# The shifted cross attention of an twelve-block decoder kernel: one head pipeline over four items instead of one per item

## The chip, the cores and the metric

The kernel runs on one core of one Trainium2 chip as one program. The metric is device microseconds (us) of one execution, the median of several. TensorE (PE, with its weight load PEld), VectorE (DVE), ScalarE (ACT), GpSimd (POOL) and SyncE (SP, whose queue issues nearly all transfers) each run their own instruction list in order and meet at semaphores.

## The reference, cut to what matters

Twelve blocks follow each other: attention, cross attention and feed-forward, in four layers, on x of 8 x 256 x 128. The change touches the cross attention of layer 1, a head attention with relative positions: the position scores `bd` are computed against all 512 positions and then shifted left row by row.

```python
def left_shift(x):
    L = x.shape[-2]
    M = x.shape[-1] - L
    flat = x.reshape(x.shape[:-2] + (-1,))
    i = jnp.arange(L)[:, None]
    j = jnp.arange(M)[None, :]
    i = jnp.arange(L)[:, None]
    j = jnp.arange(M)[None, :]
    idx = 2 * L - 1 + i * (M + L - 1) + j
    out = flat[..., idx]
    keep = j - i <= M - L
    return jnp.where(keep, out, jnp.zeros((), dtype=x.dtype))
...
ac = jnp.einsum('bhtd,bhsd->bhts', qh + b_u[None, :, None, :], kh)
bd = jnp.einsum('bhtd,hmd->bhtm', qh + b_v[None, :, None, :], ph)
scores = (ac + left_shift(bd)) / math.sqrt(D_K)
attn = jax.nn.softmax(scores, axis=-1)
out = jnp.einsum('bhts,bhsd->bthd', attn, vh).reshape(b, t, H_SIZE)
return out @ w_o
...
```

q is the layer norm of x, k and v are `ctx_1024`, and the result is added to x. There are 16 heads of width 8, and 8 batch items; positions and keys number 512 and 256, and no key is masked out.

## The kernel before

The 8 items form two streams of four (`streams`, `ITEMS` = 4); stream 0 holds the even items. Each stream has its own buffers, semaphores and four PSUM banks: S0, S1, T, V. For each engine a Python generator per stream walks the twelve blocks (the "own" walk), and a second one per stream runs ahead and prepares the next block's operands (the "ahead" walk, the `front` functions). `alternate` (line 2955) merges these four walks of an engine into one instruction list: the string `TURNS[engine]` says how many steps each walk takes in turn. So the order on every engine is fixed by those strings; a wait holds up everything behind it on that engine, of both streams.

In the shifted stage (`L1_xattn`, block 4) an item goes through these steps:

- **Front** (ahead walk, `front`, `front_norm`): layer norm, transposes, q, k and v matmuls, all in bank S1. ACT and DVE cut q with either bias and k into three bf16 pieces (`split_q`, `split_k`); SP stores them to HBM (`stack_out`, tile `stacks`) and reads them back in the layout of the matmuls (`stack_back`): `qv` (a tile `region` or `qv`, double buffered), then `qs` and `kz`, of which a stream has one copy each. So line 2745 lets SP wait until all 16 heads of the item before are scored, and then reads `qs` (96 rows of 4 KB) and `kz` (2 x 48 rows).
- **Shear**: for head h, PE multiplies `qv` with the positions into S1 (`shift`), ACT copies it to SBUF, and for each pair of heads SP stores it to HBM (`skew<-region`, two transfers) and reads it back with a row pitch one element shorter (`skew_room<-skew` and `P<-skew` in turn, two slots a stream), which is the left shift.
- **Head**: five heads behind the shear. PE forms the scores in S0, DVE adds the shifted part and takes the maximum (line 2090), ACT exponentiates (`P<-P,negm`), PE transposes into T (line 1153), DVE copies T out (line 2160), and every four heads PE weighs v into V.
- **End** (`finish`): PE transposes the 16 heads' results into T and V (line 912), DVE takes the sums and divides (lines 2164, 1976, 1838), PE transposes (line 888), ACT copies, PE projects into S0, DVE adds to x.

An item's loop (line 1171 on PE) runs `h` from 0 to 22: the last 7 rounds have no shear, and the first 5 have no head. Then comes the end, and only then, in the same walk, the first shear of the stream's next item. The ends of the two streams' items stand less than half an item apart in the lists.

Of the kernel before, what the change touches and what calls it, by code (L numbers as in the profile page):

```python
# [12 lines left out]
ALU = mybir.AluOpType  # L13
# [4 lines left out]
TOK = S // 128  # L18
# [34 lines left out]
    "tensor": ("0100110012003211110011001300130021002100210021002100110011001300140062002100210022001500210031002100120021001200"  # L53
        "2300120040010011001001020010101100100201001101003100110010010010220011003100110011001100111011001100210033002200"
        "1100210011001300110011003100420041001110010021100200110020010100101011001100120020101300100112001001010021002101"
        "0200110012002300110012001100410010100100202011001100321021002300110021001001410030011001010011001001010011001200"
        "1200210041003100220012001100410012001100110021003100120034002100130011001100110041001100130014001100330013001300"
        "2100110021001200110033001200110011003100110012002100210011001100120021005400110011002100120023001200210021002100"
        "1200230012001200210031001100110011001200260031001200230041001200130011001200110011004200440032001200130011001100"
        "3200210012002100120022003100120023006100120024001100110011001200230041001200240011002200310012002200220032001200"  # L60
        "1400210031001100230023003200330032001100510012001200120011001100110012001100120043002300110011002200310011001100"
        "3300110022001200130011001100310011001100120021001200220031001200110012006100120024001200210012002300410012002400"
        "1100120011004200230010100120020101030010610021002300120011004300110041003200120021001100210011002100220012002100"
        "2300110022001200110011003100110011001100210012001100211010100100211011002100110020102200120020011100100101021100"
        "1400110023002100410012001100120011001200210022002100130012001200110021001100210031002100210011001100210011001100"
        "1100210012003200210022001100220011001100120011002100120021001210010010100110120011001100111001001300130012003101"
        "1100100112020300430021001100130011002100310011002100110011002100120011002400140012002100120011002100210021002200"
        "3100410012001200110021002100130011001100210011001300110011001100110021001010212012002010020021001100120011001100"
        "1100210013002200110210010200220101001100110011001100410031001100110021001100120011001100120012001200110012002100"
        "2300210022001100110041001100410011002100110021001100110021001100110011001200230022001100110011001200110012001200"  # L70
        "1100120011001100310023003100230011001100130022001200110031003200120012002100110011002200110022001100210022001300"
        "1100310031001200120013001100120021001100220012001100110011001200230021001100310022001100210012001100140041002200"
        "3100110011001200240011002200310011003100120012001200110021002100210021001100110011001300140011002100220021001210"
        "011001001410041002100210010021002100110020013001400161007002a301010011001200210012001200110023002300130011002100"
        "1100110021001200230021001100110011001200110011001100110011001100110011101100211001001200130012004100101001002100"
        "1100110015002700110021001100110101001200210012001100220021001100200111001200500132001100140011001300110011002100"
        "1100120032001100110011100100301011003300220011001010220023001100120023002601030112001100110011003200110021001001"
        "3200120041008200110014001200110013004200210011001300210011001010210030101100111011001100110011001110210011002500"
        "1100130013010201110112003101310011002100130032001300320021006100120014001100120013004100110013001100110011001100"
        "1100220011001010202001001100110021101200110013001200110021001100230014002100110011001100210013001200210012001001"  # L80
        "1100220010011001300102002100130043001300110012001100410011001100210011001100210011001100110031001100110031001010"
        "0100201010101100130022001510410022003200110022001101220011001100220011002200110010011100110010011100100112001200"
        "1200210032002100110011001100120011003100111021001100320010104100231011001100111001002100210021001200120012002100"
        "1200110021001100300102001100220011002100110011001200130012012001110021002100400111001100120012101210010012001100"
        "1310010031001100110021001100110032001200120012102110010011001100220022001010020031001101010011011100210011001001"
        "21002100110032002300202003002100101001001101120111010a100110051008011301040103003200j001610020016001910011001100"
        "41001200220011001100210011002300210041001200420018001600151004101e100f100110c1006100101041002002a00100104010p010"
        "01010201030013001200150012001500160100104100201031005100210021009100301103010500230013001c0014016100410041004100"
        "5001200141001100140011001200110013001300110011001100110112001300240012002100110012001100230033001e00150012001100"
        "2100101002001010010022100200120010200100111021003100110021101010021010100210021005001100310011004100110011010101"  # L90
        "2200100101003200210010012001030010013200310021001100100111001001410020018100200120013001510061002200110013001b00"
        "110017001a0016001x"),
    "scalar": ("0200110010111100210014002200210011004200220011001100210012001100330011002100110022001200310022001200110011001200"
        "1001001220110011002100100100110101001001110021001101201021001100120011001100100112100100501001003100101014001300"
        "2100210011004600110011001100110032001100110011002010510020011200110011002110521001001200110011001200210010101001"
        "0010330011001601110203002100120013001200210010102200110010104010410011003010410030100100110010013100510102001400"
# [423 lines left out]
def program(nc, dram, where, out):  # L520
# [183 lines left out]
    def rows_before(w, q):  # L704

        return (16 * 2 * ITEMS if q % 2 else 0) + 16 * (w * len(range(q % 2, MORE, 2)) + q // 2)
# [2293 lines left out]
```

## Time and profile before

| | us |
|---|---|
| median of 3 runs | 2091.87 |
| lowest, highest | 2087.24, 2092.49 |
| the profiled execution | 2096.31 |
| its span, first to last instruction | 2094.5 |

| engine | busy us | share of the span |
|---|---|---|
| PE | 1745.7 | 83% |
| PEld | 1356.6 | 65% |
| DVE | 1438.9 | 69% |
| ACT | 1035.9 | 49% |
| POOL | 461.7 | 22% |

A row of a view of windows gives, for one stretch of the span, its length, each engine's busy time with the number of instructions, the granted clock of TensorE as a share of full speed, the mean busy share of the 16 DMA engines, and what they moved. A timeline row gives the start and the length, and in brackets how long the engine sat idle before it and what released it. The mean granted clock of the whole span is 0.925.

### The profile page before, as it was taken

The numbers are of one execution on the slowest core, as the hardware profiler recorded it, in microseconds if no ns is written. First come the engines' busy times: TensorE is split into PE (matmuls) and PEld (weight loads), VectorE is DVE, ScalarE is ACT, GpSimd is POOL, SyncE is SP. The second block draws the span as 40 slices with busy tenths as digits, with TensorE's granted clock in tenths as the row PEclk, the third lists the DMA queues.
The fourth block names the chain that finished last, engine by engine and source line by source line (L and its number), as shares of the span: only waits on it lengthen the run. The fifth ranks groups of instructions, "written<-read, shape, count | busy, mean of one in ns | idle before, by whom it ended". The sixth has DMA issues, their size and how long they took to land.

```text
span 2094.5 us, 39958 instructions
## 1 busy us (share of the span) xinstructions
PE 1745.7 (83%) x14536; PEld 1356.6 (65%) x14536; DVE 1438.9 (69%) x4894; ACT 1035.9 (49%) x2588; POOL 461.7 (22%) x448
## 2 busy tenths in 40 slices
PE   6588999999998677779998798899878867766885
PEld 5455687776776455546887576667658855654785
DVE  6689524777877579779888677767864456567643
ACT  3277525666765556656333354455434335631342
POOL 3300110000002000000546200000464544213442
PEclk9899999999999789989999899999989879976888
DMA  5334067000001988885201323323126543332356
GB/s 179 79 74 117 16 240 231 1 1 1 1 1 37 269 214 238 245 225 152 81 1 28 90 72 89 89 59 88 48 77 190 161 120 93 77 139 84 103 153 199
DMA packets 211051, 228.56 MB, mean 109 GB/s; under 512 B 16052, under 2 KB 179276, under 8 KB 210216
## 3 DMA queue, kind: packets, MB, share of 16 engines
q1 hardware_dynamic: 205864, 215.71, 36.3%
q0 software_dynamic: 4992, 10.30, 1.4%
q8 instruction: 116, 1.90, 0.4%
q14 instruction: 79, 0.65, 0.1%
HBM read 130.57 MB, written 94.98 MB: 108 GB/s over the span
## 4 chain that ended last, share of the span: by engine, by line
PE 49%; DVE 22%; DMA 11%; ACT 7%; issue 6%; POOL 2%; SPq 2%; another core or an unknown queue 0%; DVEq 0%; ACTq 0%; POOLq 0%
PE banks L746 42%; ACT P L1512 4%; PE banks L1061 3%; DMA stacks<-region 3%; SPq L2680 2%; DVE region L1918 2%; DMA back<-mask,block_to 2%; DVE P L1838 2%; DVE negm L1849 2%; DVE P L2090 1%; ACT region L1512 1%; DVE route L1838 1%; DVE region L2160 1%; DVE region L1838 1%; PE banks L1153 1%
## 5 line engine op out<-in xcount | busy, mean ns | idle before, releaser
L2504 POOL TENSOR_TENSOR norms<-norms,consts 128x2 f32<-128x2 f32 x112 | 81.6, 730 | 1224.2 <-DVE norms L1842 1223.8
L1512 ACT ACTIVATE P<-P,negm 128x256 f32<-128x256 f32 x512 | 240.8, 498 | 114.0 <-DVE negm L2110 64.7
L1512 ACT ACTIVATE P<-banks 128x512 f32<-128x512 f32 (+2 forms) x392 | 188.4, 511 | 164.9 <-PE banks L746 155.6
L1849 DVE TENSOR_REDUCE negm<-banks 128x2 f32<-128x512 f32 (+1 forms) x264 | 149.2, 591 | 34.9 <-PE banks L746 31.1
L1512 ACT ACTIVATE region<-banks 128x384 f32<-128x384 f32 (+4 forms) x221 | 108.5, 506 | 78.1 <-PE banks L746 55.4
L746 PE MATMUL banks<-kz,qs 128*128 128x256 bf16 (+1 forms) x512 | 122.5, 275 | 27.2 <-DMA kz<-stacks 9.9
L746 PE MATMUL banks<-bands,identb 128*128 128x160 bf16 (+1 forms) x768 | 142.4, 247 | 0.0
L746 PE MATMUL banks<-xnT,region 128*128 128x256 f32 x544 | 138.8, 389 | 3.2 <-ACT xnT L1512 3.1
L746 PE MATMUL banks<-region 64*128 64x256 f32 (+6 forms) x922 | 124.6, 356 | 9.9 <-ACT region L1512 4.1
L746 PE MATMUL banks<-qv,region 128*128 128x256 bf16 (+2 forms) x512 | 114.9, 266 | 18.6 <-ACT P L1512 15.4
L746 PE MATMUL banks<-qs,kz 128*128 128x256 bf16 (+2 forms) x512 | 112.1, 262 | 17.7 <-ACT P L1512 8.9
L746 PE MATMUL banks<-kz,region 128*128 128x256 f32 x512 | 121.9, 384 | 4.0 <-DVE skew_room L1838 2.8
L2583 POOL DMA_INDIRECT back<-mask,block_to x92 | 89.4, 972 | 120.7 <-DVE mask L2338 110.1
L746 PEld LDWEIGHTS banks<-xnT,region 128*128 128x128 f32 x544 | 99.4, 194 | 21.4 <-ACT xnT L1512 6.9
L746 PEld LDWEIGHTS banks<-kz,region 128*128 128x128 f32 x512 | 95.6, 191 | 19.9 <-DVE skew_room L1838 5.1
L1838 DVE TENSOR_TENSOR P<-P 128x512 f32<-128x512 f32 (+1 forms) x136 | 84.6, 663 | 30.2 <-ACT P L1512 29.2
L746 PEld LDWEIGHTS banks<-region 128*128 128x128 f32 (+3 forms) x922 | 79.9, 160 | 36.8 <-issue 14.9
L746 PE MATMUL banks<-P,region 128*32 128x256 f32 (+6 forms) x1408 | 93.3, 325 | 10.4 <-ACT P L1512 3.7
L2110 DVE CUSTOM_DVE_ANT_0 P<-banks,region 128x256 f32<-128x256 f32 x256 | 92.7, 420 | 9.4 <-PE banks L746 9.2
L746 PE MATMUL banks<-region,identb 128*128 128x256 bf16 x384 | 98.2, 284 | 0.0
L746 PE MATMUL banks<-region,qv 128*128 128x256 bf16 (+2 forms) x384 | 79.2, 269 | 22.6 <-DMA qv<-stacks 9.6
L1153 PE MATMUL banks<-perm,P 128*128 128x128 f32 x512 | 82.2, 290 | 18.6 <-ACT P L1512 9.2
(288 smaller groups left out, 4485.2 us busy)
## 6 DMA issues: line engine op xcount, KB each, us to landing
stacks<-region SPq DMA_DIRECT2D x178, 192.0 KB, 3.0
sorted<-qs SPq DMA_DIRECT2D x4, 4160.0 KB
skew<-region SPq DMA_DIRECT2D x64, 256.0 KB
qs<-stacks SPq DMA_DIRECT2D x24, 384.0 KB
kz<-stacks SPq DMA_DIRECT2D x48, 192.0 KB
skew<-region SPq DMA_DIRECT2D x64, 128.0 KB
skew_room<-skew SPq DMA_DIRECT2D x32, 256.0 KB
P<-skew SPq DMA_DIRECT2D x32, 256.0 KB
```

The lines of the kernel that those rows point to most:

```text
L746: return p.e.matmul(o, lhsT, rhs, start=start, stop=stop)
L1061: i = p.e.transpose(s.T[:, k * S + t * 128:k * S + (t + 1) * 128], s.P[:, n // 2 % 2, n % 2, t, k * 128:(k + 1) * 128], ident)
L1153: m = p.e.transpose(s.T[:, k * S + t * 128:k * S + (t + 1) * 128], s.P[:, i % 2, 0, t, k * 128:(k + 1) * 128], ident)
L1512: return a.e.activation(o, i, f, **kw)
L1838: return v.e.tensor_tensor(o, a, b, op)
L1849: return v.e.tensor_reduce(o, a, AX, op, negate=negate)
L1918: step(v.e.tensor_copy(dst, t.unsqueeze(1).to_broadcast([128, dst.shape[1], S])))
L2090: m = v.e.tensor_tensor_reduce(Pq[:, t, :], bank[:, t * S:(t + 1) * S], addend(t), -1.0, 3.0e38, ALU.add, ALU.min, s.negm[:, t, i:i + 1])
L2110: m = v.e.tensor_tensor_reduce(Pq[:, t, :], s.bank[par][:, t * S:(t + 1) * S], rel[:, h, 128 - 128 * t:128 - 128 * t + S], -1.0, 3.0e38, A ...
L2504: g.e.tensor_tensor(room[:, :, 0], room[:, :, 0], pows[:, :], ALU.pow).then_inc(done, 1)
L2583: g.e.indirect_dma_start(s.back[:, :], to, s.block_y[:, n % 2, :], None).then_inc(s.stored[n % 2], 16)
L2680: d.e.dma_start(dst, src).then_inc(sem, 16)
```

## The change

On every engine, `L1_xattn` now does nothing for three of a stream's four items and runs one loop over all 64 heads at the first (`c` from 0 to 73). Shears of the next item follow those of the last one without a pause. The item's end becomes three steps, `heads_turned`, `out_turned` and `projected`, laid after the third, fourth and fifth head round of the next item; they use T and V, never S0, and a buffer `O4` of their own. The front of the next item is laid on the heads 3, 5 and 8 of the running item (`SLOTS`): it takes bank S1 in turn with the shears, so PE waits there for ACT and DVE to empty it. `qs` and `kz` come back in two halves: pairs 0 to 3 once the running item's first 8 heads are scored, pairs 4 to 7 once all 16 are, on a semaphore of their own. The `TURNS` strings of all five engines were made anew, for the whole kernel.

```diff
+    SLOTS = (3, 5, 8)
+
+    def last_of(c):
+        return c % H == H - 1
...
+            def shift(c):
+                k, h = divmod(c, H)
+                qv = s.qv_of[k % 2]
+                yield
...
+                if k + 1 < ITEMS and h in SLOTS:
+                    front, m = j + k + 1, FRONT_SEQ.index(j + k + 1)
+                    if h == SLOTS[0]:
+                        p.wait_ge(s.f_out, out_before(front) + 1)
+                    elif h == SLOTS[1]:
+                        p.wait_ge(s.q_out, m + 1)
+                        p.wait_ge(s.k_out, m + 1)
+                    else:
+                        p.wait_ge(s.f_out, out_before(front) + 2)
                 p.clear(s, "S1")
...
+            def score(c):
+                k, h = divmod(c, H)
+                yield
+                p.wait_ge(s.stack_in, back_before(j + k) + 64)
+                if h >= H // 2:
+                    p.wait_ge(s.stack_rest, 48 * (k + 1))
+                p.clear(s, "S0")
...
-            for h in range(H + 7):
-                if h < H:
-                    yield from shift(h)
-                now = h - 5
...
-            p.clear(s, "V")
-            yield from finish(s, j, W1["L1x_o"], None, ("T", "V"), ("S0", 0))
+            for c in range(H * ITEMS + 10):
+                now = c - 5
+                if c < H * ITEMS:
+                    yield from shift(c)
+                if 0 <= now < H * ITEMS:
+                    yield from score(now)
+                if 3 <= now - 2 < H * ITEMS and (now - 2) % 4 == 3:
+                    yield from weigh(now - 2)
+                if 0 <= now - 1 < H * ITEMS:
+                    yield from turn(now - 1)
+                if now >= H and last_of(now - 3):
+                    yield from heads_turned()
+                if now >= H and last_of(now - 4):
+                    yield from out_turned()
+                if now >= H and last_of(now - 5):
+                    yield from projected()
...
+        def half_back(s, i0, sem):
+            qs, kz, pairs = s.qs_of[4][0], s.kz_of[4][0], slice(i0, i0 + PAIRS // 2)
+            d.wait_ge(s.stack_out, d.now(s.stack_out))
+            d.wait_ge(s.rooms_clean, ROOMS[4][0])
+            q_rows, k_rows = (s.via[k].rearrange("(r i s) -> r i s", i=PAIRS, s=S)[0:AUG, pairs] for k in range(2))
+            dma(qs[0:AUG, pairs], q_rows, sem)
+            for par in range(2):
+                at = slice(HALF * par, HALF * (par + 1))
+                dma(kz[at, par, pairs], k_rows[at], sem)
...
                 yield
+                d.wait_ge(s.heads_out, H * ITEMS + max(H * k - H // 2, 0))
+                d.wait_ge(s.stack_in, back_before(j) + 16)
+                half_back(s, 0, s.stack_in)
+                yield
                 d.wait_ge(s.heads_out, H * (ITEMS + k))
-                d.wait_ge(s.stack_in, back_before(j) + 16)
-                yield from q_back(s, j)
-                yield from k_back(s, j)
+                half_back(s, PAIRS // 2, s.stack_rest)
...
-    "tensor": ("0100110012003211110011001300130021002100210021002100110011001300140062002100210022001500210031002100120021001200"
+    "tensor": ("0500510012002400130010105300410010010200240013006200110031001200250012006200210011001200240011001100400100120033"
```

What this moves on PE, at the end of stream 0's first item. Names end in the stream's number; `P_n` under lines 1153 and 1147 is a head's transpose, `kz_n,qs_n` with `identb` a head's score, `region1,v_n` the weighing, `region1,region2` (128x128 and 128x256) a shear of the second item, `OTp_n` the first step of the end, `xn_0` the second, `region1,OT_0` the projection, `region1,ctxT_0` the v matmul of a front. Before:

```order
L746 MATMUL banks_0<-region1,v_0 32x256 x8
L912 MATMUL banks_0<-perm,OTp_0 128x128 x8
L746 MATMUL banks_1<-kz_1,qs_1 128x256
L746 MATMUL banks_1<-region1,identb 128x256
L746 MATMUL banks_1<-kz_1,qs_1 128x256
L746 MATMUL banks_1<-region1,identb 128x256
L746 MATMUL banks_1<-region1,v_1 32x256 x8
L888 MATMUL banks_0<-perm,xn_0 128x128 x2
L1153 MATMUL banks_1<-perm,P_1 128x128 x4
L746 MATMUL banks_0<-region1,OT_0 128x128 x2
L746 MATMUL banks_0<-region1,region2 128x128
L746 MATMUL banks_0<-region1,region2 128x256
```

Now:

```order
L709 MATMUL banks_0<-region1,ctxT_0 128x128 x2
L1171 MATMUL banks_0<-perm,OTp_0 128x128 x8
L709 MATMUL banks_1<-region1,region2 128x128
L709 MATMUL banks_1<-region1,region2 128x256
L709 MATMUL banks_1<-kz_1,qs_1 128x256
L709 MATMUL banks_1<-region1,identb 128x256
L709 MATMUL banks_1<-kz_1,qs_1 128x256
L709 MATMUL banks_1<-region1,identb 128x256
L1147 MATMUL banks_1<-perm,P_1 128x128 x4
L709 MATMUL banks_0<-region1,region2 128x128
L709 MATMUL banks_0<-region1,region2 128x256
L709 MATMUL banks_1<-region1,region2 128x128
```

Before, the three steps of the end stand close together and stream 0's next shear comes behind the last of them. Now only the first step stands here, shears of both streams and a whole head of stream 1 follow it at once, and a front's matmul of stream 0 is ahead of it.

On SP, around the return of stream 0's second `qs` and `kz` (`stacks_n<-region2` is `stack_out`, `skewN<-region1` a shear's store, `skew_room` and `P` its return). Before:

```order
L2680 DMA stacks1<-region2 64x6x256 x2
L2680 DMA stacks0<-region2 64x6x256 x2
L2680 DMA skew0<-region1 128x2x128
L2680 DMA skew0<-region1 128x2x256
L2680 DMA qs_0<-stacks0 96x2048
L2680 DMA kz_0<-stacks0 48x2048 x2
L2680 DMA ctxT_0<-in_ctxT 128x256
L2680 DMA stacks1<-region2 64x6x256 x2
L2680 DMA skew_room_0<-skew0 128x2x128
L2680 DMA skew_room_0<-skew0 128x2x256
L2680 DMA skew0<-region1 128x2x128
L2680 DMA skew0<-region1 128x2x256
```

Now:

```order
L2708 DMA skew1<-region1 128x2x128
L2708 DMA skew1<-region1 128x2x256
L2708 DMA qs_0<-stacks0 96x1024
L2708 DMA kz_0<-stacks0 48x1024 x2
L2708 DMA stacks1<-region2 64x6x256 x2
L2708 DMA skew0<-region1 128x2x128
L2708 DMA skew0<-region1 128x2x256
L2708 DMA skew_room_1<-skew1 128x2x128
L2708 DMA skew_room_1<-skew1 128x2x256
L2708 DMA qs_0<-stacks0 96x1024
L2708 DMA kz_0<-stacks0 48x1024 x2
L2708 DMA ctxT_0<-in_ctxT 128x256
```

The return was one group of three transfers with 2048 elements a row; it is now two groups with 1024, and between them stand shear transfers of both streams and a store of stream 1. SP issues 24 transfers more in all (924 for 900 in the walks). On each engine outside this stage the same instructions stand in nearly the same places: blocks begin and end within some tens of instructions of where they did.

## Rows read from the trace of the kernel before

**Rows 1.** Windows of the shifted stage: stretch, length, busy us, clock, DMA share, GB/s.
```profile
700.00:740.00 40.00, 33.24 (x276) 24.11 (x280) 30.33 (x115) 26.88 (x66) 0.01 (x1) 0.87 0.95 279
740.00:780.00 40.00, 29.97 (x225) 19.69 (x224) 29.45 (x92) 19.39 (x44) 0.80 (x1) 0.79 0.80 205
780.00:820.00 40.00, 32.53 (x308) 24.16 (x312) 34.92 (x132) 31.08 (x76) 0.70 (x1) 1.00 0.86 242
820.00:860.00 40.00, 26.98 (x220) 18.38 (x212) 29.03 (x96) 21.27 (x49) 1.50 (x2) 0.92 0.86 227
860.00:900.00 40.00, 35.53 (x320) 26.31 (x320) 35.36 (x129) 29.01 (x70) 0.00 (x0) 0.95 0.88 251
900.00:940.00 40.00, 28.83 (x214) 18.35 (x218) 28.37 (x99) 23.11 (x52) 2.79 (x4) 0.86 0.82 215
940.00:960.00 20.00, 18.53 (x173) 13.61 (x164) 17.11 (x69) 16.09 (x39) 0.00 (x0) 0.94 0.96 281
960.00:983.00 23.00, 20.27 (x190) 14.28 (x191) 20.86 (x85) 13.98 (x33) 1.39 (x2) 1.00 0.47 134
```

**Rows 2.** Windows of first to last shear store, of all before, all after.
```profile
688.00:971.00 283.00, 219.18 (x1837) 153.26 (x1838) 218.17 (x773) 181.70 (x424) 7.14 (x10) 0.89 0.86 238
0.00:676.00 676.00, 602.80 (x4256) 449.32 (x4256) 468.10 (x1532) 381.18 (x964) 71.57 (x78) 0.98 0.25 74
983.00:2094.00 1111.00, 912.29 (x8348) 746.80 (x8348) 737.56 (x2536) 466.37 (x1185) 379.52 (x356) 0.91 0.34 96
```

**Rows 3.** Timeline of SyncE's issues: start, length, engine, line, transfer.
```profile
688.52 1.64 SPq L2680 DMA_DIRECT2D skew<-region  x2
...
749.67 1.64 SPq L2680 DMA_DIRECT2D skew<-region  x2
...
765.56 0.88 SPq L2680 DMA_DIRECT2D skew<-region  x2
...
971.02 0.87 SPq L2680 DMA_DIRECT2D skew<-region  x2
```

**Rows 4.** Waits of TensorE, 688 to 983: who waited for whom, us, times, longest.
```profile
PE banks L746 <- DMA kz<-stacks: 9.9, 2, 9.3
```

**Rows 5.** Waits of SyncE, 688 to 971.
```profile
SPq L2680 <- DMA skew<-region: 35.6, 34, 2.6
SPq L2680 <- DVE region L1838: 25.9, 12, 3.8
SPq L2680 <- ACT region L1512: 14.6, 18, 2.0
SPq L358 <- DVE negm L2090: 6.3, 8, 2.9
```

**Rows 6.** Timeline of VectorE at the end of stream 1's first item.
```profile
776.17 0.19 DVE L2164 COPY sums<-banks 128x32 f32<-128x32 f32 x1 [5.12 <-PE banks L912]
776.40 0.35 DVE L1976 RECIPROCAL rec<-sums 128x32 f32<-128x32 f32 x1
776.79 0.42 DVE L1838 TENSOR_TENSOR xn<-banks,rec 128x256 f32<-128x256 f32 x1
779.25 0.42 DVE L1838 TENSOR_TENSOR x<-x,banks 128x256 f32<-128x256 f32 x1 [2.04 <-PE banks L746]
```

**Rows 7.** Issues of line 2680, 685 to 975: duration ns min/median/max, span.
```profile
L2680 SPq DMA_DIRECT2D skew<-region x128: 359/469/1596, 688.5 to 971.4; - x128
...
L2680 SPq DMA_DIRECT2D kz<-stacks x16: 422/438/1497, 697.5 to 928.6; - x16
```

**Rows 8.** Groups of instructions, 680 to 990: count, busy us, mean ns, idle before.
```profile
L1512 ACT ACTIVATE P<-P,negm 128x256 f32<-128x256 f32 x256 | 113.9, 500 | 49.1 <-DVE negm L2090 47.8
L2160 DVE COPY region<-banks 128x512 f32<-128x512 f32 x127 | 85.3, 686 | 8.7 <-PE banks L1153 7.5
...
L746 PE MATMUL banks<-region,qv 128*128 128x128 bf16 (+1 forms) x128 | 23.3, 283 | 18.3 <-DMA qv<-stacks 9.6 <-ACT region L1512 8.5 <-DVE region L2160 0.2
```

**Rows 9.** DMA packets, 700 to 960.
```profile
DMA packets 81523, 62.41 MB, mean 240 GB/s; under 512 B 4879, under 2 KB 79480, under 8 KB 81496
```

More of the change, by code:

```diff
@@ L704, in rows_before @@
     def rows_before(w, q):
[L706 removed]
+        return (48 * ITEMS + 16 * 2 * ITEMS if q % 2 else 0) + 16 * (w * len(range(q % 2, MORE, 2)) + q // 2)
     BIASES = [10, 12]
@@ L1145, in shift @@
                 p.fill(s, "S1", s.shift_out)
+            def score(c):
[5 more added lines that the diff above has]
+                p.clear(s, "S0")
+                for t in range(TOK):
+                    o = s.S0[:, t * S:(t + 1) * S]
+                    mm(o, qs[:, h // 2, t * 128:(t + 1) * 128], kz[:, h % 2, h // 2, :], True, False)
+                    i = mm(o, identb[:, :], L1x_mask[:, t, :], False, True)
+                i.then_inc(s.to_vector, 1)
+                p.fill(s, "S0", s.heads_out)
             def turn(i):
@@ new lines, in out_turned, with projected @@
+            def out_turned():
+                yield
+                p.clear(s, "V")
+                for t in range(TOK):
+                    i = p.e.transpose(s.V[:, t * 128:(t + 1) * 128], s.O4[:, t, :], ident)
+                i.then_inc(s.T_full, 1)
+                p.fill(s, "V", s.T_out)
+            def projected():
+                yield
+                p.clear(s, "V")
+                for t in range(TOK):
+                    i = mm(s.V[:, t * D:(t + 1) * D], s.OT[:, 0, t * 128:(t + 1) * 128], W1["L1x_o"])
+                i.then_inc(s.to_vector, 1)
+                p.fill(s, "V", s.x_done)
@@ L1694, in L1_xattn @@
         def L1_xattn(s, b, j):
-            pairs_out = [a.now(z) for z in s.lane_out]
-            for h in range(H + 7):
-                if h < H:
+            if j % ITEMS:
+                return
+            for c in range(H * ITEMS + 10):
+                now = c - 5
+                if c < H * ITEMS:
                     yield
                     a.wait_ge(s.to_scalar, a.next(s.to_scalar))
-                    if h < 2 and j == 4 * ITEMS:
+                    if c < 2:
                         yield
@@ L1981, in finish @@
             yield
-            yield from normalise(s, j, extra, room)
+            yield from normalise(s, s.O[j % 2], extra, room)
             yield
@@ L2820, in L1_xattn @@
         def L1_xattn(s, b, j):
-            heads = H * ITEMS + H * (j % ITEMS)
-            for h in range(H + 7):
-                pair, slot = h // 2, h // 2 % 2
-                if h < H:
+            if j % ITEMS:
+                return
+            for c in range(H * ITEMS + 2):
+                if c < H * ITEMS:
                     d.next(s.shift_out)
-                if h < H and h % 2:
+                if c < H * ITEMS and c % 2:
+                    slot = c // 2 % 2
                     yield
@@ L2843, in L1_xattn @@
                         yield
-                        d.wait_ge(s.heads_out, heads + 2 * (pair - 1))
+                        d.wait_ge(s.heads_out, H * ITEMS + 2 * (pair - 1))
                     for t in range(TOK):
```

318 lines of the change are left out of this document (147 added, 171 removed).

## The prediction

> **What bounds the kernel now.** I read the windows of the shifted stage first. Its eight items run as four rounds of two (one of each stream), and the rows of [rows 1] alternate: in 740 to 780, 820 to 860 and 900 to 940, where the rounds meet, PE is busy 27 to 30 of 40 us, DVE 28 to 29, and the DMA engines 0.80 to 0.86; between them (780 to 820, 860 to 900) PE has 32.5 and 35.5, DVE 34.9 and 35.4, DMA 0.86 and 0.88, and at the two ends of the stage (700 to 740 and 940 to 960) DMA reaches 0.95 and 0.96 with 279 and 281 GB/s. The granted clock drops where the rounds meet, to 0.79, 0.92 and 0.86 of full speed, between its levels of 1.2 and 2.4 GHz, after PE has idled there. So no engine bounds the whole stage, but the transfers are nearest to it: over the 283 us from the first shear store to the last, DMA is busy 0.86, PE 219.2 us (0.77), DVE 218.2 (0.77), ACT 181.7 (0.64) [rows 2]. 238 GB/s at 0.86 makes 277 GB/s at a full share.
>
> Then the timeline of SP [rows 3]: 64 shear stores (two transfers each, 128 in [rows 7]), one for each pair of heads of each item. The sixteenth is issued at 749.67 and the seventeenth at 765.56: 15.9 us without one, where the mean of all 63 steps is (971.02 - 688.52) / 63 = 4.48 us. That is the round boundary: the pipeline of a stream empties before the next shear. The other two boundaries show in the windows. DVE sits 5.12 us idle before an end's sums and 2.04 us before the addition to x [rows 6]: the steps of the end are a chain over PE, DVE, PE, ACT, PE, DVE with nothing of their own stream beside it.
>
> **What the change removes.** The empty pipeline at three boundaries. In terms of the transfers, which it does not reduce: 283 us x 0.86 = 243 us of all DMA engines at work stay. The length of this stretch is 243 over the mean share that the new order holds. By the row of the meeting rounds (0.80 to 0.86, mean 0.83) nothing is won; by the row of full rounds with a front beside them (0.88) it is 276 us, 7 less; by 0.96, the row with no round ending in it, it is 253, 30 less. The new order has shears all the time as in 940 to 960, but it also has the stores and returns of the next item's parts with their waits for ACT and DVE, as in 860 to 900. I take the value near the middle, 0.93, because the two rows of 0.95 and 0.96 contain all kinds of this traffic (the first has the parts of both first items) and the 0.88 is what an item shows that is already draining at its end: 243 / 0.93 = 261 us, **22 us less**.
>
> Would another engine stop it earlier? DVE has 218 us of work; its best rows are 34.9 and 35.4 of 40 us (0.88), which gives 218.2 / 0.88 = 248 us: below 261, so DVE is not the bound, but it is close, and it caps the gain at 283 - 248 = 35 us. PE: 35.5 of 40 (0.89), 219.2 / 0.89 = 246 us at a mean clock of 0.89, less at a higher one. ACT has room.
>
> **What it adds.**
> Fronts in the shear bank. A front holds S1 for its transposes, its q and k matmuls and its v matmuls until ACT and DVE have emptied it, and PE waits there with both streams' work behind it. A shear needs S1 for two matmuls of 283 ns [rows 8] and one ACT copy of about the 0.50 us of an exponential, some 1.1 us of the 261 / 32 = 8 us that a stream has for a pair, or 4.1 us for a head. So S1 is free three quarters of the time, three front pieces per item find room, and the shears are five heads ahead of the heads. Cost 0; if that cover is gone, each of the 6 fronts x 3 pieces delays a shear by one emptying of about 0.5 us, 9 us.
>
> Ends among heads. The three steps take T and V, and a head's transpose takes T too: its copy is 0.686 us [rows 8]. An end's sums, reciprocal and product are 0.19 + 0.35 + 0.42 us [rows 6], once per 16 heads of 4.1 us. Waits of the end are now covered by the next item's heads; 0. Without cover: 6 ends x (5.1 + 2.0) = 43 us in both streams, about half of it in the path, which is the state before.
>
> Halves. 24 transfers more on SP. At 438 ns for an issue like them [rows 7] this is 10.5 us of SP's time. SP issues 128 of the shear stores at 469 ns (60 us), as many returns and some 70 others, in all near 157 us of 283, and its four largest waits are 35.6 + 25.9 + 14.6 + 6.3 = 82 us [rows 5]. 157 + 82 + 10 = 249 of 261: SP has little slack, but most of those waits are for what the same pair has to deliver. Cost between 0 and 10 us; I take 0 because the first half now goes while the running item still has 8 heads to do. The wait of 9.3 us for `kz` in [rows 4] is that of the first items, when there is nothing to hide it; it stays.
>
> Of the Trainium skill one rule speaks against the halves. In [rows 9] 79480 of the 81523 packets of this stage are under 2 KB anyway and the engines still move 277 GB/s at a full share; the returns are among the few larger ones. The Trainium skill, Perfetto Trace Analysis, DMA Optimizations, says that transfers under 2 KB have significant overhead each, and that splitting helps where DMA engines are generally idle, which they are not here. By that rule the halved rows would eat some of what the continuous shears bring; by the row they are free. No run here shows it yet.
>
> The first and last item. The filling of the stage and its last end are as they were, 0. The order of the rest of the kernel was made anew too: 676 us before the stage and 1111 us behind it [rows 2]. The lists show the same instructions in nearly the same places, so I take 0, with 6 us to each side: three thousandths of those 1787 us, about the 5.3 us by which three runs of one kernel differ.
>
> **The sum.** The profiled execution takes 2096.3 us (span 2094.5). 2096.3 - 22 = 2074.3; it lies 4.4 us above the median of the runs, 2091.9, so the median becomes **2070 us**.
>
> **Rivals.**
> (a) The stage goes as fast as its vector work lets it: 35 us less, 2057. For it: 0.95 and 0.96 in [rows 1], and a clock that rises when PE idles less. Against it: both streams' lists are fixed and some waits are always badly placed.
> (b) The boundaries fill but the share does not go past 0.88, since the full rounds before show no more than that, and halves, SP's slack and S1 cost the rest: 7 us less, 2085. For it: 0.86 and 0.88 in [rows 1] in the middle of rounds, where no end is near. Against it: there the next item's front was crowded into the last heads; now it is spread.
> (c) Slower: SP's queue is one list, and the change sets 12 returns of halves into it among the other stream's shears, each behind a wait for `heads_out`. While SP waits, no shear of either stream moves. The longest such wait now is 2.9 us, the mean 6.3 / 8 = 0.8 us [rows 5]. At 0.8 us the 12 cost 10 us, and that is in (b). From 22 / 12 = 1.8 us each they eat the gain; at 2.9 us they cost 35 us, and the kernel is 13 us slower: 2105. For it: only one copy of `qs` and `kz` exists. Against it: the wait stands where the shears of that stream wait for the same heads anyway, since a pair's return needs the pair two before it done.
> (d) The change does not do what it says. The lists show that it does: a shear of both streams right behind the first step of an end.
>
> **How the numbers follow.** Forecast (12 to 30 us less in the stage): 0.53. (a): 0.14. (b): 0.18. (c): 0.09. The rest of the kernel turns out over 6 us worse, with the stage as forecast or as (b): 0.06. 0.3%, or 6 us, is about what a measurement of this kernel can tell from no change. Faster by more than that: the forecast and (a) whole, half of (b): 0.76. Within it: the other half of (b) and part of the last: 0.13. Slower: (c) and some of the last: 0.11. The range: at its lower end (a), 2057, with 5 us of the rest, 2052; at its upper end (b), 2085, with 4 us, 2089. Beyond it are (c) and the outer parts of (a).
>
> **What would show it.** In the profile after: no gap above 8 us between shear stores until the last; 64 stores in about 261 us; DMA share of at least 0.92 in every 40 us window of the stage until its last 30 us; the granted clock near 1.0 from 710 us on; no DVE idle of 5 us before an end's sums; first to last instruction before the stage unchanged within 3 us. SP's waits for DVE's `negm` above 20 us in sum would speak for (c), a share of 0.88 with PE waiting for S1 (`ACT region`) for (b). I would be wrong at the root if the shears became continuous and the stage kept its length, since then neither transfers nor DVE nor the empty pipeline had set it.

## The result, and the profile of the changed kernel

The changed kernel takes **2132.4 us** (median of 4 runs, 2130.6 to 2134.9), the kernel before 2090.1 beside it: ratio 1.0196, 95% interval 1.0177 to 1.0215. Forecast were 2070 us and a faster kernel; it is 42 us slower, and outside the range.

The first view to read is where the two programs stand after the same amount of work. The windows below are cut so that they hold the same number of TensorE instructions (the first x): up to the shifted stage, the stage with its surroundings, and what is left. Columns as in [rows 1]. The kernel before (its first window is in [rows 2]):

```profile
676.00:1020.00 344.00, 266.72 (x2155) 191.31 (x2154) 266.64 (x941) 204.27 (x473) 26.65 (x37) 0.89 0.78 221
1020.00:2094.50 1074.50, 876.21 (x8129) 715.95 (x8127) 704.21 (x2422) 450.47 (x1152) 363.48 (x335) 0.90 0.34 96
```

The changed kernel:

```profile
0.00:686.00 686.00, 606.35 (x4252) 447.59 (x4252) 461.24 (x1525) 381.44 (x964) 66.20 (x72) 0.98 0.24 73
686.00:1022.00 336.00, 262.39 (x2153) 192.74 (x2154) 270.77 (x951) 204.47 (x473) 30.13 (x42) 0.90 0.78 226
1023.00:2130.00 1107.00, 887.20 (x8129) 720.02 (x8127) 706.47 (x2418) 454.02 (x1152) 363.41 (x335) 0.90 0.33 93
```

Ahead of the stage the changed kernel is 10 us behind (686 for 676); in the stage it wins about 7 (337 for 344, taken to 1023); behind it 8129 TensorE instructions take 32 us more, with the same vector work (706 for 704 us). Of these 32 us TensorE is busy 11 us longer with the same instructions (887 for 876) and idle the other 21. 10 - 7 + 32 = 35, the difference of the spans (2129.7 and 2094.5). So the loss lies where the code was not changed, only the order of the lists.

The stage itself, by the windows that answer to [rows 1]:

```profile
700.00:740.00 40.00, 22.08 (x135) 13.82 (x136) 24.48 (x79) 17.89 (x43) 3.99 (x5) 0.68 0.84 235
740.00:780.00 40.00, 32.86 (x290) 23.20 (x290) 33.63 (x125) 29.64 (x71) 1.40 (x2) 0.91 0.90 257
780.00:820.00 40.00, 30.52 (x259) 22.82 (x257) 32.74 (x107) 24.11 (x58) 0.00 (x0) 0.91 0.90 249
820.00:860.00 40.00, 31.83 (x272) 22.39 (x273) 32.70 (x118) 27.44 (x65) 1.40 (x2) 0.90 0.95 276
860.00:900.00 40.00, 35.55 (x331) 27.19 (x330) 37.82 (x129) 29.89 (x72) 0.00 (x0) 0.97 0.87 245
900.00:940.00 40.00, 34.09 (x323) 25.07 (x322) 32.72 (x124) 29.00 (x69) 1.40 (x2) 0.96 0.89 256
```

The alternation of [rows 1] is gone: between 740 and 940 the DMA share stays at 0.87 to 0.95, and nothing falls to 0.80; only the filling, 700 to 740, has 0.84. SyncE's first and last shear stores, and the one after the filling, against [rows 3]:

```profile
697.94 3.54 SPq L2708 DMA_DIRECT2D skew<-region  x4
...
709.54 0.89 SPq L2708 DMA_DIRECT2D skew<-region  x2
...
965.72 0.93 SPq L2708 DMA_DIRECT2D skew<-region  x2
```

From 697.94 to 965.72 are 268 us where there were 282.5. The gaps of 15.9, 16.4 and 13.7 us at the round boundaries are gone; the longest are 11.6 us in the filling (the second row above), 9.6 and 9.3. An end now stands within the heads of the next item, and DVE does not wait for it (no bracket behind the sums, where [rows 6] has 5.12 us):

```profile
871.39 0.42 DVE L2114 CUSTOM_DVE_ANT_0 P<-banks,skew_room 128x256 f32<-128x256 f32 x1
871.74 0.08 DVE L2114 DVE_READ_ACCUMULATOR2_ANT negm<- 128x1 f32 x1
871.74 0.19 DVE L2188 COPY sums<-banks 128x32 f32<-128x32 f32 x1
871.96 0.35 DVE L2000 RECIPROCAL rec<-sums 128x32 f32<-128x32 f32 x1
872.35 0.42 DVE L1859 TENSOR_TENSOR region<-banks,rec 128x256 f32<-128x256 f32 x1
```

And two waits of TensorE in the stage, against [rows 4]. The one for `kz` (9.9 us before) is nearly gone, and one has come that the trace before does not show there:

```profile
PE banks L709 <- DMA ctxT<-in_ctxT: 9.2, 3, 4.1
PE banks L709 <- DMA kz<-stacks: 0.5, 1, 0.5
```

### The profile page after: what moved, and what is told of

It is laid out like the page before. It is cut to its first block, busy times and chain, and to the rows that moved or that the text cites. A ratio compares the mean times of both kernels' runs of the same rounds, so it can differ in the third digit from the quotient of the medians.

```text
span 2129.7 us, 39997 instructions
## 1 busy us (share of the span) xinstructions
PE 1756.9 (82%) x14536; PEld 1361.2 (64%) x14536; DVE 1439.1 (68%) x4894; ACT 1040.7 (49%) x2590; POOL 460.7 (22%) x448
## 4 chain that ended last, share of the span: by engine, by line
PE 49%; DVE 26%; DMA 10%; ACT 5%; issue 4%; POOL 3%; SPq 3%; another core or an unknown queue 1%; DVEq 0%; ACTq 0%; POOLq 0%
PE banks L709 42%; DMA stacks<-region 3%; SPq L2708 3%; PE banks L1027 2%; ACT P L1529 2%; DVE region L1942 2%; POOL route L2684 2%; DVE region L1859 2%; DVE negm L1870 2%; DVE P L1859 1%; DVE P L2114 1%; DVE route L1859 1%; DMA back<-mask,block_to 1%; DVE P L2134 1%; DMA skew<-region 1%
## 5 line engine op out<-in xcount | busy, mean ns | idle before, releaser
L709 PE MATMUL banks<-xnT,region 128*128 128x256 f32 x544 | 144.1, 398 | 5.4 <-ACT xnT L1529 3.4
L709 PE MATMUL banks<-region 128*32 128x256 f32 (+6 forms) x922 | 124.0, 351 | 10.1 <-DVE region L2355 2.3
L709 PE MATMUL banks<-qs,kz 128*128 128x256 bf16 (+2 forms) x512 | 114.0, 264 | 13.7 <-ACT P L1529 9.9
L709 PE MATMUL banks<-maskT,identb 128*128 128x256 bf16 x384 | 96.1, 282 | 0.0
```

The source lines that it names most:

```text
L709: return p.e.matmul(o, lhsT, rhs, start=start, stop=stop)
```

## The experiments

Theory: the stage gains what was forecast or somewhat less, and the newly merged order around it costs more than it gains. Rival: the stage's own changes (fronts in S1, ends among heads, the streams' new distance at its end) delay the rest. The kernels ran in groups, each on one chip with the kernel before beside it: e1 to e4, e5 and e6, e7 to e10, e11 to e13, e14 and e15. Ratios are to the kernel before of the group. The chips differ (it took 2077 to 2093 us), so between groups a size is known as a ratio, by the medians or by traces, and where these disagree all are given. Where the edit is one of the lists, what a list says is given in words, since its characters tell nothing.

### The order ahead and behind, each alone

e1: the changed code and its order within the stage; outside it, the order of before.

```diff
 TURNS, all five engines:
-    steps outside L1_xattn as in the changed kernel
+    steps outside L1_xattn as in the kernel before
```

> The changed kernel's code, with its new order inside the shifted stage only; before and behind the stage every engine's list is that of the kernel before. In the two profiles the same instruction stands 13 us later in the changed kernel when the stage begins, 5 us earlier when it ends, and 35 us later at the end of the program. Theory 1 (the new order outside the stage costs 13 + 40 us, the pipeline itself gains about 18): 2090 - 18 = 2072 us, faster than both kernels. Theory 2 (the new stage leaves something behind, a semaphore, a buffer or 24 more transfers, that slows the rest): the stretch behind the stage stays 40 us longer, 2115 to 2120 us.

e2: as e1, with the new order behind the stage.

> As e1_old_outside, but behind the shifted stage the lists are those of the changed kernel; before it those of the kernel before. Theory 1: e1 + 40, 2112 us, and the stretch behind the stage again 40 us longer. Theory 2: like e1, within 5 us. If the loss sits in the lists before the stage and is only passed on, it would also be like e1.

e3: the code of before, with the new order ahead of the stage alone.

> The kernel before, with the changed kernel's lists up to the first own step of the shifted stage and nothing else of the change. Theory 1: 12 to 13 us slower than the kernel before, 2103 us, all of it ahead of the stage. If the order is worth nothing there (and the 13 us came from elsewhere): 2090 us.

| kernel | median us | ratio, 95% | against its base |
|---|---|---|---|
| before (same chip) | 2086.4 | | |
| e1 | 2074.6 | 0.9945, 0.9924 to 0.9966 | -12 |
| e2 | 2111.9 | 1.0118, 1.0093 to 1.0143 | +37 over e1 |
| e3 | 2102.8 | 1.0071, 1.0047 to 1.0096 | +16 over before |

-12 + 37 + 16 = 41, where the whole change made +42. The traces of the whole change gave +10 and +32 for the two outer stretches, so each part is known to some 6 us. e1 was run twice more, on two other chips:

> e1 once more (the order of before outside the shifted stage, of after inside it), as the anchor of the three kernels beside it and of e5 and e6, whose kernel before took 2076.6 us where that of e1 took 2086.4. Theory (differences add up stretch by stretch): ratio to before 0.9945 as in e1, about 2075, and e5 and e6 then are 12 and 22 us slower. If the ratio comes out near 1.000 instead, the gain of the stage was a matter of the chip.

> e1 once more as the anchor of e14: 0.994 of the kernel before.

It gave 2080.8 us and 0.9942 (0.9921 to 0.9963), and 2068.3 us and 0.9943 (0.9926 to 0.9961). The windows of its first trace, cut as above; the first is again 676 us for 4256:

```profile
676.00:1007.00 331.00, 259.97 (x2152) 190.88 (x2153) 267.38 (x941) 204.20 (x473) 26.63 (x37) 0.91 0.79 224
1007.00:2076.70 1069.70, 868.10 (x8130) 707.66 (x8128) 702.66 (x2422) 451.67 (x1152) 363.56 (x335) 0.91 0.34 96
```

The stage takes 331 us for 344, 13 less (its other two traces take 329 and 336 us for as many instructions), and what is behind it does not suffer (1069.7 for 1074.5). The rival falls. e2, with the new order behind:

```profile
676.00:1010.00 334.00, 261.68 (x2153) 192.33 (x2154) 267.02 (x945) 204.35 (x473) 27.18 (x37) 0.90 0.78 222
1010.00:2110.80 1100.80, 879.64 (x8129) 712.70 (x8127) 706.32 (x2418) 453.29 (x1152) 363.18 (x335) 0.90 0.33 93
```

31 us more for the same instructions. TensorE is busy 11.5 us longer with them (879.6 for 868.1) at a granted clock of 0.90 for 0.91, and idle 20 us longer. So about a third of the loss shows as slower matmuls, and the rest as waiting.

### Is it one place or many

e5 takes the new order behind the stage up to about 1500 us only, e6 from there on only.

```diff
 TURNS, all five engines, behind L1_xattn, against e1:
-    as in the kernel before
+    e5: as in the changed kernel up to about 1500 us, then as in the kernel before
+    e6: as in the kernel before up to about 1500 us, then as in the changed kernel
```

> As e1 (the order of before outside the shifted stage, that of after inside it, 2074.6 us), but from the stage's end at about 986 us to the end of the third attention layer behind it at about 1500 us the order of after, and from there on that of before again. e2, with the order of after all the way behind the stage, was 37 us slower than e1, 12 of them there by 1500 us. Theory 1 (the loss is many small waits, each place pays for itself): this kernel loses 12 us against e1, to about 2087, and its partner e6 loses the other 25, so that the two losses add up to the 37. Theory 2 (one early wait shifts the two streams against each other and all that follows is the price): this kernel loses more than 25 of the 37, 2100 or above. Theory 3 (the seams between orders cost by themselves): e5 and e6 together lose well over 37.

> The counterpart of e5: the order of before until the end of the third attention layer behind the stage, at about 1500 us, and from there on that of after. Theory 1 (many small waits, each place pays for itself): 25 us more than e1, about 2100, with nothing lost before 1500 us and most of it between 1640 and 1720 us. Theory 2 (an early shift of the two streams carries the loss): under 12 us more than e1, 2087 or less. Theory 3: both kernels lose over 25.

e5: 2087.0 us, ratio 1.0048 (1.0032 to 1.0064), span 2092.5. e6: 2097.3 us, ratio 1.0102 (1.0078 to 1.0125), span 2095.8. Against e1's span of 2076.7 these are +16 and +19, together 35, and e2 has +34; by the medians they are +12 and +23, and e2 has +37. By these two measures the losses add up. The ratios say +21 and +33, together 54, where e2 has 36: the kernel before took only 2076.6 us on the chip of e5 and e6, and e1 was not run there. So each size is known to some 10 us, and that the seams between the orders cost something too (theory 3) is not excluded. The eight powers of GpSimd in the fronts of L3 make a landmark in every trace (first and last start; line numbers differ). e1, e5, e6:

```profile
L2712 POOL TENSOR_TENSOR route<-route,consts x8: 6740/6740/6782, 1648.0 to 1801.7; 128x40 f32<-128x40 f32 x8
```

```profile
L2700 POOL TENSOR_TENSOR route<-route,consts x8: 6741/6742/6775, 1664.8 to 1820.1; 128x40 f32<-128x40 f32 x8
```

```profile
L2705 POOL TENSOR_TENSOR route<-route,consts x8: 6740/6742/6774, 1655.9 to 1816.3; 128x40 f32<-128x40 f32 x8
```

The other two traces of e1 have the first start at 1644.7 and 1650.6, so 6 us are noise here. e5 has its whole loss before the first power (1664.8 for 1648.0) and keeps it; e6 has 8 there and 15 at the last. Both stretches of the new order lose, and neither carries the whole loss: theory 2 of both texts falls.

### Does a single wait carry it

In that stretch one wait had grown. DVE's step behind the power reads what GpSimd computes in 6.74 us, and the lists decide what DVE does meanwhile. DVE's wait for it over the whole kernel, in e1 and in e6:

```profile
DVE route L1891 <- POOL route L2712: 5.6, 5, 1.7
```

```profile
DVE route L1884 <- POOL route L2705: 16.0, 7, 6.4
```

and the place of the 6.4 us in e6, after one small copy as its only cover:

```profile
1692.13 0.49 DVE L1891 TENSOR_REDUCE route<-region 128x40 f32<-128x320 f32 x1
1692.84 0.29 DVE L2387 COPY mask<-banks 128x128 f32<-128x128 f32 x1 [0.22 <-PE banks L730]
1699.51 0.18 DVE L1884 TENSOR_SCALAR route<-route 128x40 f32<-128x40 f32 x1 [6.39 <-POOL route L2705]
```

The first try at it (e8 on e6, e9 on e1, e10 on the changed kernel) moved another step than its texts say: not the one that waits for the power but the third one behind the sum of squares, which holds the splits of q, and one step of L3's attention beside it. What the texts expect is thus not what was tested. In e8 and e10 DVE's order differs in five places, in e9 in three. Of e8, at one of its places:

```diff
-L1963 CAST region<-OT 128x768
-L1880 TENSOR_TENSOR OT<-OT,region 128x256
-L1963 CAST region<-OT 128x512
-L1880 TENSOR_TENSOR region<-OT,region 128x256
 L2456 COPY v<-banks 128x16x8 x2
 L1880 TENSOR_TENSOR region<-region 128x320
 L1891 TENSOR_REDUCE route<-region 128x40
+L1963 CAST region<-OT 128x768
+L1880 TENSOR_TENSOR OT<-OT,region 128x256
+L1963 CAST region<-OT 128x512
+L1880 TENSOR_TENSOR region<-OT,region 128x256
```

> e6 (order of after from 1500 us on) with one step moved, in DVE's list alone: the step of the third L3 front that waits for the GpSimd power (6.74 us for one, eight of them) comes up to three turns of other work behind the step that hands the power its data, where after's list has it right behind it in most of the eight. In e6 DVE waits 16.0 us for it in 7 places, the longest 6.4 us, and in e1 5.6 us in 5. Theory 1 (this wait at the head of DVE's list is on the path; both streams' work is queued behind it): 8 to 10 us less than e6, about 2088, DVE's wait for the power near 6 us. Rival (DVE has slack there, and the wait is paid for by what comes late anyway): within 3 us of e6.

> The reverse of e8, made on e1: in DVE's list alone, the eight steps that wait for the GpSimd power go right behind the step that hands it its data, with no turn of the other stream between. Each of the eight waits can then be up to 6.7 us. Theory 1: DVE's waits for the power rise from 5.6 us towards 8 x 6.4 = 51 us and the kernel loses a good part of it, 15 to 45 us over e1, 2090 to 2120. Rival (slack): within 3 us of e1.

> The changed kernel itself with the edit of e8 and nothing else. Its DVE waits 16.6 us for the power in 8 places, the longest 6.6. Theory 1: 8 to 10 us less than the changed kernel, about 2123. Rival (slack): 2132.

e8: 2122.7 us, 1.0140 (1.0122 to 1.0159), span 2122.6: 27 over e6 by the spans and 25 by the medians, though 8 by the ratios, and e6 was not run on e8's chip. e10: 1.0283 (1.0251 to 1.0316), 17 to 18 over the changed kernel by either. e9, the step pulled forward on e1: 0.9945 (0.9921 to 0.9970) beside e1's 0.9942, nothing. So a few steps of one engine, moved by at most three turns in five places, with every other list as it was, cost between 8 and 27 us. How is argued and not shown: the splits feed `stack_out`, and SP's returns stand behind it. In e8 ACT's wait for those stores, 1650 to 1900 us, is

```profile
ACT region L1550 <- DMA stacks<-region: 18.7, 7, 4.8
```

where e6 has 3.5.

Then the step that does wait. e11 on e6 and e12 on the changed kernel, one place:

```diff
 L1891 TENSOR_REDUCE route<-region 128x40
 L2387 COPY mask<-banks 128x128
+L1888 SCALAR_TENSOR_TENSOR x<-kz,place_w,x 128x128 x8
 L1884 TENSOR_SCALAR route<-route 128x40
...
-L1888 SCALAR_TENSOR_TENSOR x<-kz,place_w,x 128x128 x8
 L1915 BN_STATS norms<-x 128x6 x2
```

e13 on e1: the step right behind the sum of squares in all eight places.

```diff
 L1898 TENSOR_REDUCE route<-region 128x40
-L1895 SCALAR_TENSOR_TENSOR x<-kz,place_w,x 128x128 x8
-L1922 BN_STATS norms<-x 128x6 x2
-L1925 BN_AGGR norms<-norms 128x2 x2
-L1891 TENSOR_SCALAR norms<-norms 128x2
 L1891 TENSOR_SCALAR route<-route 128x40
```

> e6 with one step moved, in DVE's list alone: the eight additions to x (one group of 2.4 us, from L1888, that in the order of before lie between the sum of squares and the step that waits for the GpSimd power) go ahead of that step again, in the one place where DVE waits 6.4 us for the power; in e6 they stand right behind it. All other lists and seven of the eight places are as in e6. Theory 1 (the wait is on the path): DVE's wait there falls from 6.4 to 4 us or less, everything behind it comes 2.4 us sooner, and if the PE block that waits for the additions (kz, OT of the experts) also comes sooner, up to 6. Profile span 2090 to 2094 against 2095.8. Rival (slack, or the next wait takes its place): within 1 us at the instructions that follow. Rival 2, from e8 and e10: what waits for the rotated q and k (PE's transposes of skew_room, 7.9 us in one place) comes later by the 2.4 us and costs as much: slower by 2 or more.

> The changed kernel with the edit of e11 and nothing else (DVE waits 6.6 us there). As e11: by theory 1 2.4 to 6 us less than the changed kernel's span of 2129.7, by the rival no change, by rival 2 2 or more us slower.

> e1, the order of before outside the shifted stage, with the step that waits for the GpSimd power pulled right behind the sum of squares that hands it the data, in all eight places of DVE's list (the edit that e9 was meant to be). One power is 6.74 us, and DVE then can wait for nearly all of it each time: the waits for it go from 5.6 us to up to 50. Theory 1: the kernel loses 60% or more of what the waits grow by, since both streams' work stands behind them: 25 to 50 us, 2100 to 2125. Rival (DVE has slack in this stretch, being busy 85 of 140 us): under 5 us over e1.

e11: 1.0099 (1.0068 to 1.0130), e6 had 1.0102. e12: 1.0229 (1.0189 to 1.0268), the changed kernel had 1.0196. No gain in either, though the wait did fall in both, in e12 from 16.6 to 10.0 us and in e11 from 16.0 to 8.9:

```profile
DVE route L1884 <- POOL route L2705: 8.9, 7, 2.1
```

7.1 us of waiting taken away, nothing won; that the next late thing took its place is argued, no run shows which. e13: 2136.0 us, 1.0267 (1.0236 to 1.0298), span 2133.0 against 2075.4 in the second trace of e1 and 2074.5 in the third: 58 us by the spans, 68 by the ratios, with this wait:

```profile
DVE route L1891 <- POOL route L2712: 54.9, 8, 6.9
```

49 us more of waiting (54.9 for 5.6) in one list cost 58 to 68 us. So the wait is on the path once it is bare everywhere, and DVE has no slack to swallow it; but the 10 us of it that the new order added are not what it loses by.

### Which part of the stage's change gains

e4 is e1 with both halves of `qs` and `kz` issued together, after all 16 heads of the running item. The transfers themselves stay the same halves, so e4 tests when they start and not how large they are.

```diff
-                d.wait_ge(s.heads_out, H * ITEMS + max(H * k - H // 2, 0))
-                d.wait_ge(s.stack_in, back_before(j) + 16)
-                half_back(s, 0, s.stack_in)
                 yield
                 d.wait_ge(s.heads_out, H * (ITEMS + k))
+                d.wait_ge(s.stack_in, back_before(j) + 16)
+                half_back(s, 0, s.stack_in)
                 half_back(s, PAIRS // 2, s.stack_rest)
```

> As e1_old_outside, but qs and kz of an item come back together, both halves behind the wait for all 16 heads; the front half is issued where the rear half is, so SP never waits for 8 heads. If the halves matter: PE waits at the first heads of items 2 to 4 for a return of 5 to 9 us in each stream, partly beside the other stream, 5 to 20 us slower than e1. If they only cost SP (the rival of my prediction): 0 to 5 us faster than e1.

2093.8 us, ratio 1.0031 (1.0013 to 1.0049), 19 us over e1, and its stage is 350 us for 331 (676 to 1026, as many instructions). Without the early half the continuous pipeline is no faster than the kernel before, by the ratio 0.3% slower. TensorE waits for the return again, 7.1 us up to 905.8 and 9.5 us up to 933.8:

```profile
PE banks L737 <- DMA kz<-stacks: 16.6, 2, 9.5
```

and SyncE has a gap between shear stores like the old ones, 17.3 us from 925.32 to 942.60:

```profile
925.32 2.65 SPq L2736 DMA_DIRECT2D skew<-region  x4
...
942.60 1.65 SPq L2736 DMA_DIRECT2D skew<-region  x3
```

(The order was laid for halves; with one laid for a whole return, e4 might lose less.)

### The stage's new wait

e14 is e1 with the load of the next item's `ctxT` taken out of the next front, where SP's list has it behind the second half, and put behind the first half.

```diff
             if n in LOADED:
                 yield
-                d.wait_ge(s.f_full, full_before(j))
-                dma(s.ctxT[:, :], dram["ctxT"][b], s.loaded)
+                if n != 4 or k == 0:
+                    d.wait_ge(s.f_full, full_before(j))
+                    dma(s.ctxT[:, :], dram["ctxT"][b], s.loaded)
...
                 half_back(s, 0, s.stack_in)
+                if k + 1 < ITEMS:
+                    d.wait_ge(s.f_full, full_before(j + 1))
+                    dma(s.ctxT[:, :], dram["ctxT"][own_batches[s.n][k + 1]], s.loaded)
                 yield
```

> e1 with SP's load of the next item's context (ctxT, fronts of items 2 to 4 of both streams) issued right behind the first half of the running front's qs and kz, instead of at the head of the next front's own list behind the second half. In e1 PE waits 10.0 us for it in three places of the shifted stage, the longest 4.5 us at 701 to 706 us in the filling, where nothing else is under way. Theory 1 (on the path): PE's wait for ctxT goes to under 2 us and the kernel gains 4 to 10 us over e1, near 2068. Rival (the filling then waits for the next thing, a return of qs and kz or the vector work): under 2 us at the stage's end.

2062.0 us, ratio **0.9914** (0.9888 to 0.9939), where e1 beside it (its third run) has 2068.3 and 0.9943. Theory 1: TensorE waits 0.2 us for `ctxT`, and the stage is 326 us for 331:

```profile
PE banks L737 <- DMA ctxT<-in_ctxT: 0.2, 1, 0.2
```

```profile
676.00:1002.00 326.00, 258.48 (x2146) 191.62 (x2147) 266.64 (x940) 204.08 (x472) 26.24 (x36) 0.92 0.79 228
```

The two intervals overlap a little; the medians differ by 6 us and the traces by 12, of which 2 lie ahead of the edit. So the gain is likely, and its size is known only roughly. This kernel is the best of the study, 0.9% under the kernel before.

## Why the prediction was wrong

- **The step that failed** is the last one before the sum: the rest of the kernel at 0 with 6 us to each side. It was argued from lists that "show the same instructions in nearly the same places", and sized by the spread of one kernel's runs. Measured are +16 ahead and +37 behind, in sum 53 us, by e1 to e3. The traces of the whole change have 10 and 32. The same instructions a few turns apart are not the same order: e8, e10 and e13 move DVE's steps in five to eight places and cost between 8 and 68 us. The case "the rest turns out over 6 us worse" was given 0.06.
- **The stage, 22 us less:** right in kind, high in size. e1 gives 12 by the medians and 13 by the windows (15 and 8 in its other traces); with `ctxT` out of the way 17 and 18. The 64 stores take 268 us for the forecast 261. Two terms of that sum were off, in opposite directions. The share of the DMA engines was put at 0.93 and is 0.88 from 697.94 to 965.72 us, what rival (b) had. And the 243 us of DMA work did not stay: 268 x 0.88 is 236, since the engines moved 251 GB/s at 0.88, or 285 at a full share, for 277 before. So the stage came out between the forecast and (b), partly by luck.
- **The cap by DVE, 35 us at a share of 0.88:** the cap was not reached, but the share that it was worked out from was not DVE's best. e1 has a window with 39.36 of 40:

```profile
780.00:820.00 40.00, 35.84 (x356) 27.77 (x355) 39.36 (x139) 31.19 (x75) 0.70 (x1) 1.00 0.95 266
```

- **Fronts in S1, 0:** missed was the DMA that a front issues. Its load of `ctxT` now stands behind the second half in SP's list, TensorE waits 8 to 11 us for it, and that is worth about 6 us (e14). Missed too was a wait in the filling: TensorE stands 6.2 us for DVE before the transposes of a front, up to 707.33 us, which the kernel before does not do there. No run prices it. More waiting for S1 to be emptied does not show: from 686 to 1005 us TensorE waits 8.1 us for ACT's copies (`ACT region`), where the kernel before has 12.1.
- **Ends among heads, 0:** right, DVE waits 0.3 us before the sums in the stage, where it waited 8.7.
- **Halves, 0 to 10 us of cost:** wrong in sign. In this order they carry the gain: 19 us (e4). With continuous shears and a late return TensorE stands at the boundary for `kz`, 7.1 and 9.5 us. The prediction read the 9.3 us of [rows 4] rightly as the wait of the first items (it ends at 703.34 us), but it did not stay: in the changed kernel the filling has the waits for DVE and for `ctxT` (4.1 us) instead. The rule of the Trainium skill that was set against the halves (Perfetto Trace Analysis, DMA Optimizations) names transfers under 2 KB, and the benefit of splitting where DMA engines are idle. The halved rows are 2 KB, just not under it, and no run here prices them, since e4 keeps them. The same section of the Trainium skill says that splitting may allow some transfers to start sooner. With that the 19 us agree, though the DMA share here was 0.87 to 0.95.
- **Rival (c), SP's list blocked:** did not happen. SP waits 6.7 us for DVE's `negm` in the changed kernel and 6.3 before [rows 5], where over 20 would have spoken for it. Its mechanism showed elsewhere: the load of `ctxT` stood behind another transfer's wait in SP's one list.
- **The signs to look for:** gaps of 9.6 and 9.3 us against the 8 allowed, DMA at 0.87 to 0.95 from 740 us on and 0.84 before it, against 0.92, a clock of 0.90 to 0.97 (0.68 in the filling) against "near 1.0". "Unchanged within 3 us before the stage" was the sign that mattered, and it read 10.

What stays open is which waits the new order loses by. It is spread over at least three stretches: 16 us ahead of the stage (medians of e3), and by the traces 16 from its end to 1500 us and 19 from there on. The one wait that stood out was not it. Exchanging the whole list of a single engine wasn't tried, since the lists of the five engines must fit each other.

## What to carry to other kernels

When a change makes an order anew, it is two changes: price them apart, and put the old order back wherever the code did not change. A re-merged list of the same instructions is not neutral; here it cost 53 us around a stage that gained 12. And a new pipeline should be followed by the list of new waits in its own stage: one load that stood behind a wait it did not need kept back about 6 us where 12 had been won.

## What the runs showed beyond that

- Taking 7.1 us off DVE's wait for the power gained nothing (e11), while adding 49 us of the same wait cost 58 to 68 (e13). The worth of a wait in a kernel with five fixed lists is not its length. Here a single one was worth nothing, and eight together cost more than their own length. The granted clock was lower beside that (0.916 for 0.930 over the whole kernel), and how much of the cost is the clock's was not measured.
- One unchanged kernel differs between chips by more than many of these effects: the kernel before has the medians 2076.6, 2079.0, 2082.5, 2086.4, 2090.1 and 2093.1 us beside the kernels of this study (2079.0 and 2082.5 on one chip). The ratio of e1 to it held at 0.9942 to 0.9945 on three chips.
